# Attention B: the rows of maxima go straight from SBUF into the stacked operand, on ScalarE's queue

## The reference, cut to what matters

```
# per sequence, 16 heads of width 8, segments of 64 tokens, 4 segments
scores = q @ k.T / sqrt(8); scores = where(causal, -inf, scores)     # 64 x 64 inside each segment
A_dot  = softmax(scores) @ v
A_mem  = (sigma(q) @ M) / (sigma(q) . z + eps)                       # memory of the earlier segments
out    = (beta * A_mem + (1 - beta) * A_dot) @ W_o.T
M, z   = M + sigma(k).T @ (v - V_prev), z + sum(sigma(k))            # sequential over the segments
```

## Time and profile before

| | before |
|---|---|
| median of 3 runs | 2139.34 us |
| profiled execution | 2121.74 us, span 2120.0 us |
| mean granted clock of TensorE | 0.854 |
| PE / PEld busy | 1713.4 / 1420.0 us |
| DVE / ACT / POOL busy | 1494.4 / 764.9 / 842.8 us |
| DMA | 159.66 MB, mean 75 GB/s; q1 (SP) 22.6%, q10 (ACT) 0.2% of 16 engines |
| c_q_st<-scratch_c_m_dram, SP | x64, 12.0 KB each |
| scratch_c_m_dram<-c_mt, ACT | x64, 12.0 KB each |

### The profile page before, as it was taken

One profiled execution on the slowest core, in us unless ns is written; L12 is line 12 of the kernel. 1 busy time (PEld: TensorE's weight loads), 2 busy tenths in 40 slices (PEclk: granted clock), 3 DMA queues, 4 the chain that ended last, 5 costly groups with the idle time before them and its releaser, 6 DMA issues. The chain is left out here.

```text
span 2120.0 us, 45990 instructions
## 1 busy us (share of the span) xinstructions
PE 1713.4 (81%) x13668; PEld 1420.0 (67%) x13668; DVE 1494.4 (70%) x3615; ACT 764.9 (36%) x1663; POOL 842.8 (40%) x1054
## 2 busy tenths in 40 slices
PE   5999999999999999947665577787787887787787
PEld 3888888888888888845554355565565665665665
DVE  5678888888888888848885556665666666656655
ACT  1455555555555555522222122222222222222222
POOL 3445544455444455436564423232322232223331
PEclk8999999999999999968886677877887777777868
DMA  3322222222122222123331222222222222212221
GB/s 115 115 93 78 72 72 73 71 71 71 68 73 71 73 73 74 61 66 99 90 97 44 77 66 67 82 75 75 71 72 72 80 75 76 69 66 79 81 70 41
DMA packets 181309, 159.66 MB, mean 75 GB/s; under 512 B 10417, under 2 KB 162609, under 8 KB 181234
## 3 DMA queue, kind: packets, MB, share of 16 engines
q1 hardware_dynamic: 178930, 157.95, 22.6%
q10 hardware_dynamic: 2304, 0.79, 0.2%
HBM read 113.87 MB, written 44.83 MB: 75 GB/s over the span
## 5 line engine op out<-in xcount | busy, mean ns | idle before, releaser
L600 PE MATMUL a_bank<-a_vp,a_prob 128*128 128x96 f32 x4096 | 546.4, 278 | 0.3 <-ACT a_prob L457 0.3
L600 PEld LDWEIGHTS a_bank<-a_vp,a_prob 128*128 128x128 f32 x4096 | 512.8, 197 | 16.8 <-ACT a_prob L457 8.6
L633 DVE TENSOR_REDUCE a_nmax<-a_bank 128x2 f32<-128x512 f32 x512 | 331.7, 686 | 119.2 <-PE a_bank L527 118.8
L457 ACT ACTIVATE a_prob<-a_bank 128x512 f32<-128x512 f32 x512 | 306.0, 598 | 179.3 <-PE a_bank L582 170.5
L1429 ACT ACTIVATE c_prob<-c_bank 128x256 f32<-128x256 f32 x256 | 98.8, 386 | 353.0 <-PE c_bank L1510 317.9
L1707 DVE TENSOR_REDUCE c_nmax<-c_bank 128x4 f32<-128x512 f32 x256 | 168.8, 686 | 69.2 <-PE c_bank L1530 68.7
L527 PE MATMUL a_bank<-a_k_st,a_q_st 96*128 96x256 bf16 x1024 | 208.2, 286 | 7.7 <-DVE a_nmax L633 5.0
L1560 PE MATMUL c_o_bank<-c_vb,c_prob 128*128 128x96 f32 x1024 | 209.1, 339 | 2.3 <-DVE c_ad L1832 1.3
L582 PE MATMUL a_bank<-a_q_st,a_k_st 120*128 120x256 bf16 x1024 | 202.8, 280 | 0.0
L1506 PE MATMUL c_bank<-c_causal_t,c_ident 128*128 128x256 bf16 x256 | 84.9, 332 | 120.6 <-DMA c_q_st<-scratch_c_m_dram 113.8
L1560 PEld LDWEIGHTS c_o_bank<-c_vb,c_prob 128*128 128x128 f32 x1024 | 172.2, 239 | 10.1 <-ACT c_prob L1429 3.0
(11 more groups left out here) (195 smaller groups left out, 3141.6 us busy)
## 6 DMA issues: line engine op xcount, KB each, us to landing
a_q_st<-scratch_a_parts_dram SPq DMA_DIRECT2D x192, 96.0 KB
a_k_st<-scratch_a_parts_dram SPq DMA_DIRECT2D x64, 288.0 KB
c_q_st<-scratch_c_parts_dram SPq DMA_DIRECT2D x192, 96.0 KB
c_k_st<-scratch_c_parts_dram SPq DMA_DIRECT2D x64, 288.0 KB
scratch_a_parts_dram<-a_parts SPq DMA_DIRECT2D x32, 384.0 KB, 2.7
scratch_c_parts_dram<-c_parts SPq DMA_DIRECT2D x32, 384.0 KB, 3.0
a_x<-in_x SPq DMA_DIRECT2D x32, 128.0 KB, 10.7
scratch_y<-a_y SPq DMA_DIRECT2D x32, 128.0 KB, 9.4
```

Source lines behind the costliest of these rows:

```text
L457: act.activation(prob[h % 4][:, :, :].rearrange("p a b -> p (a b)"), t_ps[h % 2][:, :], ACT.Exp).then_inc(exped, 1)
L600: mm = pe.matmul(o_ps[g % 2][:, at:at + VC], prob[h % 4][:, c, t * P:(t + 1) * P], vp[o][:, c, :], start=c == 0, stop=c == NT - 1)
L633: dve.tensor_reduce(nmax[:, t, 2 * g:2 * g + 2], s_ps[t][:, :].rearrange("p (h k) -> p h k", h=2), AX.X, ALU.max, negate=True).then_inc(ma ...
```

## The change

The maxima no longer pass through DRAM. Where ScalarE issued one DMA of `mt` to DRAM, it now issues three, one for each bf16 part: 8 partitions of 512 B of `mt` go into one partition (8 heads x 256 tokens, 4 KB) of `q_st`. Each adds 16 to `m_in`, and PE waits for 48 a batch. `shift_rows` is gone from SP's list, so `stack(1)` follows `stack(0)`; since the halves of two batches can now be in flight together, `stack_in` gets one semaphore for each buffer. ScalarE's copy to `mt` waits until the three DMAs of the batch before have landed.

```diff
-        stack_in = [sem(f"stack_in{i}") for i in range(2)]
+        stack_in = [[sem(f"stack_in{i}{k}") for k in range(2)] for i in range(2)]
...
-                def shift_rows(h2):
-                    b, o = n - 1, 1 - i
-                    sp.wait_ge(mt_out, (2 * b + h2 + 1) * 16)
-                    apart(sp, spare)
-                    sp.dma_start(q_st[o][MROW:KROWS, h2 * H // 2:(h2 + 1) * H // 2, :],
-                                 m_dram[o, h2].rearrange("(a h) t -> a h t", a=NPART)).then_inc(m_in[h2], 16)
...
                     stack(0)
-                if active(j, u, 1):
-                    shift_rows(0)
-                    shift_rows(1)
-                if active(j, u, 0):
                     stack(1)
...
                             if later(j, b, 1):
-                                act.wait_ge(mt_out, (2 * b + h2 - 1) * 16)
+                                act.wait_ge(m_in[h2], b * MI)
                             act.copy(mt[h2][:, :], mt_ps).then_inc(mt_d, 1)
                             act.wait_ge(mt_d, 2 * b + h2 + 1)
-                            if h2 or later(j, b, 1):
-                                act.wait_ge(mt_out, (2 * b + h2) * 16)
-                            act.dma_start(m_dram[1 - i, h2], mt[h2][:, :]).then_inc(mt_out, 16)
+                            for a in range(NPART):
+                                act.dma_start(q_st[1 - i][MROW + a:MROW + a + 1, h2 * H // 2:(h2 + 1) * H // 2, :],
+                                              mt[h2][a * H // 2:(a + 1) * H // 2, :]
+                                              ).then_inc(m_in[h2], 16)
...
-                            pe.wait_ge(m_in[g // (ST // 2)], (b + 1) * 16)
+                            pe.wait_ge(m_in[g // (ST // 2)], (b + 1) * MI)
...
-                            pe.wait_ge(stack_in[q // 2], (b + 1) * 4 * 16)
+                            pe.wait_ge(stack_in[o][q // 2], (pair(j, u, 1)[0] + 1) * 4 * 16)
```

More of the change, by code:

```diff
@@ L1166, in attention_b @@
         mp_d = sem("mp_d")
-        mt_p, mt_d, mt_out = sem("mt_p"), sem("mt_d"), sem("mt_out")
+        mt_p, mt_d = sem("mt_p"), sem("mt_d")
         m_in = [sem(f"m_in{i}") for i in range(2)]
@@ L1194, in attention_b @@
         x_dram, out_dram, wc_dram = pairs(d["x2"]), pairs(d["out"]), d["folded"]
-        parts_dram, m_dram = d["c_parts_dram"], d["c_m_dram"]
+        parts_dram = d["c_parts_dram"]
         flat = lambda a: a[:, :, :].rearrange("p c f -> p (c f)")
         N_LOAD, N_LATE, SPLIT, MP, AD, VD = 3, 4, 4, 8, 6, 4
+        MI = NPART * 16
         MT_AT = (3, 7)
@@ L1273, in stack @@
                                      .unsqueeze(0).broadcast_to([NPART, HD, H // 2, T])
-                                     ).then_inc(stack_in[h2], 16)
+                                     ).then_inc(stack_in[i][h2], 16)
                     sp.dma_start(k_st[i][0:SROWS, hs, :],
```

## The result

The changed kernel takes 1978.72 us (1974.56 to 1981.11, four runs) against 2139.44 us: ratio 0.9241, 95% interval 0.9219 to 0.9264. The forecast was 1974, with 1938 to 2038 as its range. The profiled execution took 1979.98 us, span 1978.2 us, mean granted clock 0.889 against 0.854.

A forecast was written before the change was run, and what follows sets the result against it. PE was held by the late return of the maxima from DRAM and the half clock after it. 29.12 - 3.66 - 2.0 = 23.5 us a batch, taken as 23.6, gains 165 us: 2139.3 to 1974 us, range 1938 to 2038.

The forecast's parts named there:

- Part 1: PE's wait for the maxima of g = 0: rows land 3.6 us ahead of need, removing all 3.66 us a batch.
- the margin: Maxima rows of g = 0: forecast to land at 1514.8, 3.6 us before PE needs them.
- Part 2: TensorE's clock: recovers once the idle stretch goes, 2.0 us a batch; low bound 0, high bound 5.0.
- the second slow stretch: TensorE at clock 0.50 for 6.3 us from 1522.6, after 4.22 us idle; expected to go with that idle stretch.
- GpSimd's vb: Filled until 1526.45, 2.0 us after the value product; expected as the next late item, a wait of 0.5 to 1 us.
- Part 3: ScalarE: two more DMA issues each half, 2 x 0.35 = 0.7 us, with 1.6 us to spare; cost 0.
- Part 3's worst case: ScalarE issues at 0.777 us each: 1.9 us more than today's one, 0.8 us a batch, 23 us in all.
- Part 4: SP: loses two issues and a wait, stack(1) issued at about 1517 instead of 1527; by itself gives PE nothing.
- The loop through the DMAs: SP's ring from parts through stack(0), q and k copy and split: 22.9 us, claimed as the shortest possible period.
- The sum: Whole batch: 29.12 - 3.66 - 2.0 = 23.5, taken as 23.6 us; gain 165 us in all, median 1974 us.
- B: Rival: the wait goes but TensorE's clock stays at 0.77; 25.5 us a batch, 2029 us; chance 0.17.
- C: Rival: rows not free of stack traffic, stack(0) or rows 2 to 4 us later; 2044 to 2102 us; chance 0.12.

The follow-up runs named there:

- e1: Kernel before, with three direct SBUF-to-SBUF copies of the maxima instead of the trip through DRAM, still issued by SP behind stack(0): 2146.4 us, ratio 1.0038.
- e4: Kernel before, trip through DRAM kept, stacked rows reordered so each stack DMA's outermost dimension is 8 instead of 3: 1965.2 us, ratio 0.9212.
- e5: Kernel before, SP's order freed as in the change, maxima still through DRAM but store and return both on ScalarE's queue: 2046.1 us, ratio 0.9595.
- e3: Kernel before, with 14 useless matmuls in front of PE's wait for the rows of g = 0: 2101.8 us, ratio 0.9836.
- e7: Changed kernel, with three more copies of the same shape issued by ScalarE into a tile nobody reads: 2205.5 us, ratio 1.0312.
- e9: Changed kernel, with 8 useless matmuls in front of PE's wait for c_uv in slot 3: 1962.4 us, ratio 0.9232.
- e2: Changed kernel, with stack(1) held on SP until the maxima of heads 8 to 15 of the batch before have landed: 2013.5 us, ratio 0.9441.
- e6: Changed kernel, with VectorE's operations pos and neg moved from slot 1 to the end of slot 2: 1935.0 us, ratio 0.9043.
- e10: Changed kernel, with ScalarE's three issues moved behind the next exponential instead of in front of it: 1973.9 us, ratio 0.9271.

## Why the prediction was right

**The wait and its cause.** Part 1 stands: 106.0 us went to nothing. The cause it named, 576 KB ahead in SP's ring on three engines, is shown for the kernel before from both sides by e1 (copies made shorter, place kept: nothing) and e4 (place kept, stack made faster: all of it). (The 82 GB/s "without a break until 1522" is too strong for the earlier trace rows, which have 33 to 66 until 1515.75 and then 71 to 82 until about 1521; nothing hangs on it.)

What in the change removes the wait is two things. The table has the rows of heads 0 to 7, from 1210 us on: medians in us, each taken by itself, from the end of ScalarE's copy to mt and the times at which the semaphore `m_in` is full.

| | mt copied to first issue into q_st | that issue to landing | both |
|---|---|---|---|
| before | 3.7 | 7.1 | 10.5 |
| e1 | 2.7 | 7.4 | 10.2 |
| e4 | 3.9 | 2.5 | 6.3 |
| e5 | 3.5 | 4.4 | 7.8 |
| changed kernel | 0.0 | 5.4 | 5.4 |

Against e1, which has the same copies, 2.7 us are the earlier issue and 2.0 the landing. So the landing is the mis-sized term of Part 1: forecast 0.7 us for the issues and 3.0 after them, 3.7, measured 5.4 (4.0 after the last issue), and 6.8 at the longest. What saved the sum was the margin. PE starts on the rows 2.1 us after they land in the median, and 1.4 in the batch at 1511 us (forecast 3.6). Issued at once but landing as slowly as in e1, they would leave about 0.1 us (an estimate, 2.1 - 2.0); no run has that case.

**The clock.** Part 2 put 2.0 us a batch on the second slow stretch. Measured: PE busy fell by 2.6 us a batch (23.3 to 20.7) for the same work, and e3 shows that the clock follows the idle stretch, with no change to the transfers. PE's idle time fell by less than the 3.66 us of Part 1, by 2.2 us a batch (5.8 to 3.6): 0.9 us came back for c_ad, 0.4 in front of the masked scores (11.4 / 29, no releaser named) and 0.1 for the exponential. Named as late next was GpSimd's vb, with 0.5 to 1 us; the wait is there, 0.9 us (25.7 / 29), but it is for VectorE's c_ad. Both start from the same value product, and I had worked out only one.

**ScalarE.** The second mis-sized term. Part 3's cost of an issue: forecast 0.35 us with its gap, from the 0.30 of the store to DRAM, measured 0.627 (three in 1.96 us), so the exponential stands 1.6 us longer behind them and not 0.7. The time did not suffer because PE's slack was 1.6 us, and it was just used up. That this came out even is luck. (Part 3's worst case, three issues of 0.777 us, is 2.0 us more than today's one, not 1.9.) e7 and e9 show how near: with twice the issues, or a faster PE, they are on the path.

**SP.** Part 4 failed in one sentence: that the early stack(1) gives PE nothing. It gives nothing at 29 us a batch. e2 shows 35 us for it at 24. I had looked for a wait in the trace of before, where a slower batch covered it. stack(1) follows after 6.9 us, not within 6. The three engines do not carry the parts either: in the earlier trace rows the store of the parts moves at up to 287 GB/s, where the stack has 82 at most.

**The loop through the DMAs.** "A period can't be shorter than this", 22.9 us, is wrong: e6 has 17 batches of 21.5 to 22.2 us among its 29 with the same DMAs (the others go up to 25.5, and the mean is 22.85). The mis-sized term is above all the store of the parts: 4.28 us in the one batch I took, while its median from issue to landing is 3.0 us on the page of the kernel before and 2.7 on that of the changed one. With that the loop is 21.3 us. A smaller one is the 3.4 us from the first masked score to the end of the q and k copy, 2.9 in e6.

**The sum.** 23.6 us a batch forecast, 24.30 measured; 165 us forecast, 161 measured by the medians. Of the 0.7 us a batch about 0.3 are three long batches of the profiled execution (29.1, 27.1 and 25.4 us among 24.0); for the rest the 0.9 us for c_ad in place of 0.6, and the small waits named above, are at hand, but no run separates them. That the median came within 5 us of 1974 is in part luck. The profiled execution was forecast at 1957 us and took 1979.98, and between the two profiled executions the gain is 142 us. I had added 17.6 us because the profiled execution of the kernel before lay that far under its median; that of the changed kernel lies 1.3 us above its own. The two errors, some 20 us each, cancel.

**The rivals.** B (the clock does not recover) is ruled out by 0.85. C was right about one thing: another ring is not free of the stack. The copies land 5.4 us after their first issue, against 3.1 for the same copies of heads 8 to 15 in e1, which SP issues ahead of stack(1). (In C's "5 us less than what the return costs" no row has the 5: 7.56 - 4.04 is 3.5.) The Trainium skill's sentence (DMA: Bandwidth & Descriptors, "Issuing engines are not separate DMA queues"), that a second issuing engine saves only sequencer time, accounts for a part here and not for all: of the 4.8 us between e1 and the changed kernel 2.7 are the time until SP issues the rows, and 2.0 are a shorter landing of the same copies. Nor do the rows land with stack(0), which is what I took the sentence to mean: in the batch at 1511 us their semaphore is full at 1518.2, that of stack(0) at 1521.8. Its rule on the spread of a DMA ("Why a DMA increments its semaphore by 16 and not by 1") gives 8 engines in place of 3 for the stack of e4; the trace agrees in direction, 0.39 of the 16 engines busy against 0.19.

## What to carry to other kernels

A small DMA that is late is first a question of what stands ahead of it, on the engine that issues it and in its ring, and on how many DMA engines that runs; look at the outermost dimension of the large transfers before moving the small one. Count a removed idle stretch of TensorE twice, once as wait and once as the half clock behind it, and then look for who was covered by that half clock. An issue costs its queue what its own shape costs: take it from a row of the same shape, or take the dearest row at hand.

## What the runs showed that I had not expected

- A copy of 8 partitions of 512 B into one partition takes 627 ns to issue in the median on ScalarE (632 on SP in e1), against 296 for the store of 24 partitions to DRAM and 238 for its return in e5.
- A wait filled with useless matmuls is worth 36 us (e3), and in the changed kernel a clock of 0.97 (e9), which bought no time that the runs can tell.
- Once a slow stretch of 6.8 us follows each batch's wait, batches fall into step: 24.0 us in most of the changed kernel, 23.9 in e4 and e10, though e4 and e10 have different DMAs and different issues. Why this length I leave open.
